# Latent attention: where GpSimd scatters the first half of the routed rows

## What is computed

```python
x = x + 0.5 * moe8(layernorm(x))              # top-1 of 8 experts
x = x + windowed_attention(layernorm(x))      # 16 heads of 8, window 32
x = x + 0.5 * moe8(layernorm(x))
x = x + 0.5 * latent(layernorm(x))            # block B = 0
x = x + state_space(layernorm(x))
x = x + 0.5 * latent(layernorm(x))            # block B = 1

def latent(x):                                # causal, 16 heads of 8 over all 2048 tokens
    x = x + mla_attention(rmsnorm(x, norm1_w), ...)
    logits = rmsnorm(x, norm2_w) @ gate_w.T + gate_b
    top = argmax(logits)                      # one of 4 experts for each token
    return x + expert[top](rmsnorm(x, norm2_w))
```

## Time and profile before

| | us |
|---|---|
| timed runs | 1723.19, 1725.8, 1723.85; median 1723.85 |
| the profiled execution's own time | 1723.09 |
| its span, first to last instruction | 1721.8 |
| busy in the span: PE / DVE / ACT / POOL | 1243.5 / 1175.5 / 944.1 / 569.7 |
| POOL's 32 scatters into `regions` (L547) | 31.2 |
| mean granted clock of TensorE | 0.846 |

### The profile page before, as it was taken

How to read it: one execution, slowest core, us unless ns; L and a number is a source line. 1 busy time by engine, 2 the same in 40 slices (tenths; PEclk the granted TensorE clock), 3 DMA queues, 4 the chain that set the end, 5 groups by cost and what they waited for, 6 DMA issues and landing times. The chain is left out here.

```text
span 1721.8 us, 36511 instructions
## 1 busy us (share of the span) xinstructions
PE 1243.5 (72%) x13953; PEld 659.9 (38%) x13953; DVE 1175.5 (68%) x2641; ACT 944.1 (55%) x1500; POOL 569.7 (33%) x1034
## 2 busy tenths in 40 slices
PE   2665564447767788999897383876778999998746
PEld 2654454446542222223333273653222222233346
DVE  4358598625778989997873265476898999776235
ACT  1225775112345678888786241144656788887522
POOL 2331177045764321221114233375341111112323
PEclk9976665568579999999999696756999999999958
DMA  9510000021002100000000182000000000000012
GB/s 237 113 49 1 1 4 3 13 68 59 1 1 72 35 2 1 2 1 4 1 2 13 27 210 62 2 0 1 1 1 2 1 2 1 2 2 2 13 45 82
DMA packets 59133, 49.02 MB, mean 28 GB/s; under 512 B 7105, under 2 KB 54194, under 8 KB 58610
## 3 DMA queue, kind: packets, MB, share of 16 engines
q1 hardware_dynamic: 53282, 35.84, 8.1%
q0 software_dynamic: 4736, 9.74, 1.7%
q10 hardware_dynamic: 944, 1.10, 0.2%
HBM read 32.72 MB, written 18.38 MB: 30 GB/s over the span
## 5 line engine op out<-in xcount | busy, mean ns | idle before, releaser
L1795 DVE TENSOR_REDUCE arena<-psum 128x1 f32<-128x512 f32 (+4 forms) x1152 | 681.2, 655 | 153.2 <-PE psum L1609 99.1
L1740 ACT ACTIVATE arena<-psum 128x1024 f32<-128x1024 f32 (+3 forms) x640 | 558.7, 900 | 190.4 <-PE psum L1631 170.9
L1647 PE MATMUL psum<-arena 128*9 128x256 f32 (+2 forms) x4352 | 343.5, 388 | 5.4 <-issue 4.2
L1609 PE MATMUL psum<-arena 64*128 64x128 bf16 (+3 forms) x1664 | 223.8, 317 | 96.9 <-DVE arena L1795 87.1
L1631 PE MATMUL psum<-arena 64*128 64x512 bf16 (+3 forms) x1280 | 228.6, 356 | 24.5 <-ACT arena L1740 17.0
L1855 POOL TENSOR_SCALAR_AFFINE_SELECT arena<-arena 128x256 f32<-128x256 f32 x256 | 103.5, 408 | 345.9 <-ACT arena L1740 342.4
L1609 PEld LDWEIGHTS psum<-arena 64*128 64x128 bf16 x1664 | 69.3, 95 | 273.9 <-DVE arena L1795 234.0
L1631 PEld LDWEIGHTS psum<-arena 64*128 64x128 bf16 x1280 | 63.0, 94 | 178.8 <-ACT arena L1740 79.8
L1647 PEld LDWEIGHTS psum<-arena 128*9 128x9 f32 x4352 | 68.0, 88 | 161.1 <-issue 127.8
L1833 POOL CAST arena<-arena 128x16 bf16<-128x16 f32 x64 | 16.4, 257 | 285.2 <-DVE arena L1800 283.0
L679 DVE TENSOR_SCALAR small<-psum,YT 128x128 f32<-128x128 f32 x168 | 50.6, 343 | 77.0 <-PE psum L589 76.5
(11 more groups left out here) (358 smaller groups left out, 2010.7 us busy)
## 6 DMA issues: line engine op xcount, KB each, us to landing
arena<-taps SPq DMA_DIRECT2D x8, 1024.0 KB
big_w<-in_w SPq DMA_DIRECT2D x2, 2048.0 KB
ACCn<-made_rows SPq DMA_DIRECT2D x16, 256.0 KB, 3.6
regions<-sorted_rows SPq DMA_DIRECT2D x5, 741.8 KB, 4.5
sorted_rows<-arena SPq DMA_DIRECT2D x2, 1483.5 KB, 16.4
ACCn<-regions SPq DMA_DIRECT2D x32, 64.5 KB, 1.8
w<-in_w SPq DMA_DIRECT2D x2, 1024.0 KB
ACCn<-sorted_rows SPq DMA_DIRECT2D x6, 258.0 KB, 3.0
```

What stands on the lines that cost most here:

```text
L1609: mm = pe.matmul(psum[:, bank_of(("max", (v, m + r))), at:at + w], plain_q[v % 2][rows, a, i * P:(i + 1) * P], keys[rows, 2 * hq + a, key: ...
L1647: mm = pe.matmul(psum[32 * hh:32 * hh + 9, O_BANK, lo:hi], values[:, tile_of(v, j), 4 * hq + hh, :], prob[(t + hh // 2) % N_PROB][:, hh % ...
L1740: act.activation(prob[t % N_PROB][:, :, off:GW], both, ACT.Exp, scale=INV_SQRT_HD).then_inc(a_got, 1)
L1795: dve.tensor_reduce(place, rows, AX.X, ALU.max).then_inc(a_max_got, 1)
```

## The change

POOL no longer scatters the rows of tiles 8 to 15 at the event `place`. The two calls move into a function that is handed to `leave_stage`, so POOL runs them after its last instruction of the attention and after its own drain and signal, and before it waits for the other engines. PE's and DVE's parts of the event `place` stay where they are. Both latent blocks are affected, with eight scatters each.

```diff
                         if far and x in (7, 8):
                             times_c(2 * x - 14)
                             times_c(2 * x - 13)
-                    elif kind == "place":
-                        pool.wait_ge(regions_in, 16 * N_FILLS)
-                        scatter_pool(c, 0, ROUTED, ACCn, regions)
+
+            def scatter_routed():
+
+                pool.wait_ge(regions_in, 16 * N_FILLS)
+                scatter_pool(c, 0, ROUTED, ACCn, regions)
...
             attention_pool()
             if far:
                 attention_sp()
-            leave_stage()
+            leave_stage(scatter_routed)
```

## The result

The kernel with the change takes 1711.5 us (median of 4 executions, 1705.8 to 1714.1); the kernel before takes 1723.9 beside it (4 executions, 1723.2 to 1725.8). The ratio is 0.9924, 95% interval 0.9906 to 0.9942: 12.4 us, or 0.76%, faster. The prediction was 1715.6 us with a range of 1712.0 to 1724.4.

The account below looks back on a forecast made before the run. ACT running dry beside the scatters, as PE came late, was taken as the cost: 2 x (-5.1 + 1.0) = -8.2 us from 1723.09 gives 1714.9, plus 0.76 for the median, 1715.6 us; range 1712 to 1724.4.

Parts of the forecast that it names:

- POOL blocked behind its scatters costs the path next to nothing: Unit 14's first cut, behind the eight scatters: POOL late by 0.43 us, worth 0.4 us a block at most.
- PE's slow stretch: Unit 13, beside the scatters: PE's progress or signals come late and ACT idles 5.28 and 5.27 us a block.
- Removal of the slow stretch, -5.1 us a block: Unit 13: without the scatters ACT's idle time of 5.28 us goes, less 0.2 for the last score.
- the bound of 5.3: Most that removing the scatters from unit 13 could gain a block: all of ACT's idle time.
- a case to which the prediction gave 0.05: Gain a little above the bound, because PE's clock stays up where it dropped after the slow stretch; chance 0.05.
- Work queued behind the last cut, nothing: End of attention: eight scatters of 10.0 us fit POOL's 19.4 us gap before the late scatter, costing nothing.
- What the scatters meet at the end, +1.0 us a block: End of attention: PE's projection and transposes and DVE's scalings beside the moved scatters lose 1.0 us a block.
- the partial return (+3.0): Rival: PE's three steps at the attention's end each come 1.0 us late; 1719.6 us, chance 0.12.
- the slower case (+9.8 a block): Rival: at the attention's end three PE signals each come 3.26 us late; 1733 us, chance 0.10.
- the lock-out of the scalings: DVE's eight scalings at the attention's end each wait out a 0.96 us scatter, 7.7 us a block; chance 0.01.
- The rival "unchanged": Unit 13: the slow stretch belongs to PE's program there, so time stays 1723.9 us; chance 0.15.

Follow-up runs that it names:

- The extra scatters: The change, plus eight scatters of 512-byte rows of X to a spare DRAM tensor at the old place in unit 13 of each block: 1715.4 us, ratio 0.9995.
- the memsets: The change, plus eight POOL memsets without a transfer where the scatters stood, in block 1 only: 1714.1 us, ratio 0.9946.
- the same eight one unit later: Against the change, the eight scatters moved to directly behind the last cut of unit 14: 1723.9 us, ratio 0.9991 to the kernel before.
- its shifted form: The change with 56 small extra matmuls (112 PE instructions) put ahead of the stage: 1711.1 us, ratio 0.9968.
- the four forms of before: The kernel before, unchanged and with 56, 112 or 200 PE instructions added ahead: 1715.2, 1714.5, 1717.2 and 1718.2 us.
- The scatters of 4-byte rows: The change, plus scatters of 4-byte rows to a spare DRAM tensor behind unit 5, eight in block 0 and four in block 1: 1717.2 us, ratio 1.0006.

## Why the prediction was right or wrong

**The step that failed: "POOL blocked behind its scatters costs the path next to nothing", "0.4 us a block at most".** It read POOL's lateness for one cut, 931.88 less 931.45, in a schedule in which PE was late as well. The 0.43 us is what POOL was late *beyond* PE's delay, not what it would be late alone. The step had no term in the sum, so the whole gain was put on PE's slow stretch. Alone, POOL's lateness makes the stretch some 3 us longer: where the kernel before has no slow stretch, its two stretches sum to 56.8 us (mean of four kernels), those of the change to 50.6 (mean of three), which is 3.1 a block, as a mean over the clocks that these executions had. The extra scatters give 55.6 less 50.6, 2.5 a block; the memsets 4.1, or 2.9 against the change's form at their clock of 0.94; and the same eight one unit later 62.5 less 49.6, 6.5 a block. With the tails, which are 0.5 us a block shorter in the kernel before, 2.5 of the 3.1 are left. The reason is in PE's order: the weighing that needs the late cut is queued ahead of the next scores, so PE stops, ACT gets no scores, and ACT's exponentials are what the following cuts wait for.

**Removal of the slow stretch, -5.1 us a block.** The stretches shortened by 5.65 and 6.78 us, both more than the bound of 5.3, and the reason was only half right. In block 0, at nearly the same clock (0.95 and 0.93), it is the idle time and POOL's lateness of the prediction together, 5.28 + 0.43 = 5.71. In block 1 the new stretch ran at a clock of 1.00, and the change's form takes 25.4 us at 0.93: about 1.3 us of the 6.78 are the clock's, a case to which the prediction gave 0.05.

The profile of the same kernel without the slow stretch gives an estimate of the parts. Of the 6.2 us on average, 31.0 - 28.4 = 2.6 belong to the remote waits, which the kernel before shows in the first session and not later; 28.4 - 24.8 = 3.6 belong to POOL being blocked, the clock of 1.00 in block 1 counted in, and 2.8 to 3.2 of those come in the other sessions too. (These are halves of sums over both blocks: 62.0, 56.8 and 49.6 us.) So, by this estimate, about half of ACT's 5.28 us of remote idle time would have been spent on the late cuts anyway, had PE been in time; it compares executions of different sessions. The change took away two waits that cover one another: the longer hid the shorter in the trace, and the shorter is what it removes in every session.

**Work queued behind the last cut, nothing.** Right. The cover was thinner than forecast, 5.96 us in block 0, because the first scatter started 4.16 us behind the last cut; in block 1 it was 9.17. The trace calls the idle time of 4.17 us "issue", and no run here tells what it is.

**What the scatters meet at the end, +1.0 us a block.** Over-sized: the tails grew by 0.62 and 0.18 us. Two of the rivals stood on this term, the partial return (+3.0) and the slower case (+9.8 a block), and both are refuted in every profile of the change and of its shifted form (tails of 19.8 to 20.5 us). So is the lock-out of the scalings: 1.66 us with scatters beside them all along. The two terms together: 2 x (-6.2 + 0.4) = -11.6 us, where -8.2 stood: 2.2 us of the miss are in the first term, 1.2 in this one, and the 0.8 between 11.6 and the 12.4 of the medians lie outside both parts.

**The rival "unchanged"** held that the slow stretch belongs to PE's program at this place. Its time, 1723.9, is refuted by the change itself. Its own evidence turned up in another form: eight scatters at this very place, in the kernel before and in the change with extra ones, run without any remote wait in two sessions. The scatter is therefore not sufficient for the slow stretch. In the first session the slow stretch went with the scatter: with block 0 alone moved, block 1 alone kept it, in the one execution that was profiled.

**How the sizes meet the medians.** Where before has no slow stretch, stretches and tails of both blocks sum to 96.0 us (mean of the four forms of before) and to 90.9 for the three runs of the change and its shifted form, 5.1 us less; the medians say 4.8, 5.1 and 5.8. Where before has it, 11.6 and 12.4. By that the slow stretch itself makes 101.3 - 96.0 = 5.3 us of the 7 to 9 us by which the kernel before lay higher in the first comparison and the first session than later; the rest is not found.

**Open: what makes the slow stretch.** Its rows in the kernel before show PE itself standing still, and its signals late. PE's rows, then DVE's:

```profile
927.15 0.29 PE L1609 MATMUL psum<-arena 64*128 64x128 bf16 x4
928.96 0.61 PE L1647 MATMUL psum<-arena 128*9 128x256 f32 x4 [0.53 <-issue]
930.38 1.10 PE L1647 MATMUL psum<-arena 128*9 128x256 f32 x5 [0.82 <-issue]
```

```profile
933.39 0.76 DVE L1795 TENSOR_REDUCE arena<-psum 128x2 f32<-128x256 f32 x2 [5.85 <-remote]
```

PE's L1609 and DVE's row in the later profile of the same kernel:

```profile
929.36 0.29 PE L1609 MATMUL psum<-arena 64*128 64x128 bf16 x4
```

```profile
929.68 0.76 DVE L1795 TENSOR_REDUCE arena<-psum 128x2 f32<-128x256 f32 x2 [0.78 <-PE psum L1609]
```

DVE reduces what the score products of L1609 made. It started 6.24 us behind their start with the slow stretch and 0.32 us without it. ACT's exponential at 930.43 started 0.05 us behind PE's row at 930.38. So PE as a whole, its rows and its signals, came late; the readings do not separate the two.

It is not DMA traffic as such (plain copies of the same rows), and not POOL's being busy (memsets): both ran in the session that had it, and neither showed a remote wait. I then thought of a fetch of PE's instructions that meets the scatters' descriptors, and moved PE's program by 56, 112 and 200 instructions for it. The moves say nothing, since those sessions show no slow stretch even unmoved. The profiles speak against a long fetch as the cause. DMA queues of 921 to 934 us in the kernel before, with the slow stretch (share of 16 engines' time), and then in the same kernel in the fourth session, without it:

```profile
q8 instruction: 1, 0.02, 0.7%
```

```profile
q8 instruction: 1, 0.02, 0.7%
```

It is one packet, and 0.7% of 16 x 13 us, 1.5 us, in both. The scatters of 4-byte rows are the only run of the later sessions with remote waits, and there a packet did take long, between 643 and 655 us:

```profile
q8 instruction: 1, 0.02, 2.2%
```

That is 2.2% of 16 x 12 us, 4.2 us, and DVE's remote wait of 1.76 us ends at 649.7. So long packets and remote waits met once, but the slow stretch of the kernel before is there without a long packet. What makes it, and what differs between sessions, is unknown.

## What to carry to other kernels

When two engines are late at one spot, the profile shows the cost of the second only as what it adds to the first: price a blocked queue against the schedule as it would run with the other wait gone, by following what is queued in order behind the late result. A long run of queued work belongs where its queue has a gap (19.4 us here), and if it must stand elsewhere, cut it to what fits before the next result is wanted (here six of eight cost nothing that could be measured). And profile the kernel before a second time, in another session: here its time moved by 7 to 9 us, once within eight minutes and under the same chip number, and the new kernel's by one, so that the same change is worth 0.76% in the first comparison and 0.3% in two later sessions.

## What the runs showed of the hardware

- A run of eight 128-row indirect scatters holds POOL for 10.0 us, 0.96 us each (1.1 the first) with 0.30 between them, at every place where such a run stood. The same rows from SP's queue cost no engine anything that these runs show.
- A small DVE cast took 1.23 us beside a memset of POOL that had started 0.06 us before it, and 0.17 in the other block, without a memset.
- The granted clock falls for a part of the stretch in some executions, and in the change's form the length follows it: 24.15 us at 1.00, 25.4 at 0.93, 26.3 at 0.87, 27.5 at 0.84. One kernel shows both 0.87 and 1.00 in its two blocks. In the form of before, where PE waits for a late cut, it does not follow: 28.25 us at 0.84, 28.5 at 0.88 and 28.40 at 0.94. So what POOL's lateness costs shrinks from 3.0 us at 0.93 to 0.94 to 0.7 at 0.84. The two rows of the change's form furthest apart:

```profile
1595.93:1620.07 24.14, 19.64 (x226) 7.66 (x222) 5.47 (x15) 19.60 (x35) 7.53 (x21) 1.00 0.01 2
```

```profile
921.05:948.59 27.54, 23.22 (x230) 8.00 (x222) 5.48 (x15) 20.12 (x35) 7.61 (x21) 0.84 0.00 1
```

PE is busy for 19.6 us in the one and 23.2 in the other with the same matmuls (226 and 230 in the records), ACT for 19.6 and 20.1.
